# Graph layer 3: running maximum inside the gather, reciprocal in blocks beside the second pass, one message column of eight on ScalarE

## The chip, the cores and the metric

One Trainium2 chip, one of its cores. The metric is the device time of one launch in microseconds (us); lower is better. The engines are TensorE (PE in the rows; PEld is its weight load), VectorE (DVE), ScalarE (ACT), GpSimd (POOL) and SyncE (SP); SyncE and ScalarE also issue plain DMAs, GpSimd issues the indirect ones.

## The reference, cut to what matters

Four graph layers run one after the other on 3125 nodes and 100000 edges sorted by destination. The change is in the fourth, layer 3, a GATv2 attention with 4 heads of 64 numbers:

```python
def _gatv2(x, edge_index, W_l, b_l, W_r, b_r, att, bias_gat):
    xl = (x @ W_l + b_l).reshape(N, H, C)
    xr = (x @ W_r + b_r).reshape(N, H, C)
    e = jax.nn.leaky_relu(xl[src] + xr[dst], NEG_SLOPE)
    score = jnp.einsum('ehc,hc->eh', e, att)
    m = jax.ops.segment_max(score, dst, num_segments=N)
    ex = jnp.exp(score - m[dst])
    denom = jax.ops.segment_sum(ex, dst, num_segments=N)
    alpha = ex / jnp.maximum(denom[dst], 1e-16)
    out = jax.ops.segment_sum(alpha[:, :, None] * xl[src], dst, num_segments=N)
    return out.mean(axis=1) + bias_gat
```

So for each edge and head: a score, the softmax of the scores over the edges with the same destination, and the sum of the weighted source rows per destination.

## The kernel before, in words

**Layout.** Partition p holds the edges p*784 to p*784+783, one per column. Eight columns (K) are a group, 98 groups (NG) are a pass. `score` is 128 x 4 x 784: one row of 784 for each head. `f3` has the same shape.

**The gather pass** (first pass of layer 3). GpSimd fetches for each group the source rows with 8 indirect DMAs (`gather3` L814, issue at L714). SyncE loads the destination side (`load_group` L620). ScalarE writes the gathered rows out again for the second pass (`keep3a` L1087). On VectorE `edges3` (L2268) works on three groups at once: for group g it fills the destination rows column by column (`fill` L1769, instruction at L1775); for g-2 it takes the two halves that TensorE has summed (`add_up` L1338) through the leaky relu (`relu3`, L2251), adds the linear part (L2262) and reduces (L2258); for g-3 it writes the 32 finished scores (`score3`, L2266). There are 4 slots of rows: the gather of group g waits until TensorE has summed g-4 and VectorE has done both `relu3` halves of g-4, and so does SyncE's load.

**The softmax in between** is all of VectorE's steps from L2285 to L2304, one after the other (`step` waits for each): `segment_totals(6, ...)` scans the maximum forward along the columns, one scan of 784 for each head, joins the partitions and scans back; the scores less the maximum go through ScalarE's exp (L1095); `segment_totals(8, ...)` does the same with the sum. Then f3 is clamped (L2301), inverted (L2302) and multiplied into `score` (L2303), each over all 3136 columns.

**The second pass.** SyncE loads the kept rows of a group, 1 MB (`load3c` L651, four slots). The 8 columns of messages, row times weight, are made by VectorE (columns 0 to 4, KD = 5, L2322) and GpSimd (columns 5 to 7, `messages3` L822, L826) into one of two buffers `y3`. TensorE sums the four heads of the group into a PSUM bank (`head_sum` L1420, L1428, 8 recorded matmuls a group). VectorE then adds what is carried in (`sum_in`, L2033) and scans the sum of g-2 (`sum_up`, L2043) in the middle of the products of g. ScalarE copies the marks that reset the scan (L1008) and, every two groups, the finished states (`keep_states` L992, L996), and issues their DMA (L998). The products of g wait for `heads3` of g-2, which frees their `y3` buffer; `head_sum` of g waits for all products of g.

`quads` (L126) runs each pass: 6 groups written out, then a hardware loop over bodies of 4 groups. In the loop the places in `score` are computed by register instructions (DVEq, ACTq, POOLq in the rows) ahead of an instruction. `Beats` (L92) counts instructions on a semaphore; its `done` waits for the last one.

## Time and profile before

| | us |
|---|---|
| median of 3 runs | 7694.43 (7693.56 to 7702.85) |
| the profiled execution | 7678.81 |
| its span, first to last instruction | 7677.1 |
| gather pass of layer 3, 98 groups (5815 to 7078) | 1263 |
| softmax in between (7078 to 7163) | 85 |
| second pass, 98 groups (7163 to 7556) | 393 |
| rest of layer 3 (7556 to 7677) | 121 |

The profile is of one execution; stages are cut at the first and last instruction of the lines named above. "Idle before, releaser" says how long an engine had stood still before an instruction, and what ended it; "issue" is time in which nothing that the profile shows was waited for, "remote" is a semaphore event without a recorded sender.

### The profile page before, as it was taken

What the parts mean: (1) busy time and instruction counts of PE and PEld (TensorE: products, weight loads), DVE (VectorE), ACT (ScalarE), POOL (GpSimd) and SP (SyncE); (2) the same over time, 40 slices, a digit from 0 to 9 for tenths busy, and PEclk for the clock granted to TensorE, in tenths of its full rate; (3) what the DMA queues carried; (4) which work ended last, traced back from release to release, by engine and by line L of the source; (5) the groups of instructions that cost most, each with busy time, mean ns of one, the idle gap of its engine ahead of it and who ended that gap; (6) DMA issues with size and microseconds to landing.
All of it is one profiled execution on the core that took longest, in us unless ns stands there. A gap on an engine that the chain in (4) does not pass through costs nothing. (4 is left out here: it accounts for less than half of the span.)

```text
span 7677.1 us, 62689 instructions
## 1 busy us (share of the span) xinstructions
PE 2797.3 (36%) x10695; PEld 1388.6 (18%) x10695; DVE 3910.7 (51%) x10477; ACT 1035.7 (13%) x2409; POOL 3543.8 (46%) x3645
## 2 busy tenths in 40 slices
PE   2116200156600000290003333333345566555695
PEld 1114100012200000280001111111122222222232
DVE  4127200499700000299865455555545666666995
ACT  0000000012100000281352111111110000000232
POOL 5650577300177777400002655555536566654453
PEclk9999999987755555595556666666677877877897
DMA  8100000046321111100242656565637777776593
GB/s 310 44 22 13 10 1 0 0 180 231 115 85 47 47 47 47 26 0 0 101 148 71 227 198 202 196 206 193 203 110 241 243 246 244 248 245 208 208 332 117
DMA packets 458298, 1038.78 MB, mean 135 GB/s; under 512 B 129581, under 2 KB 247829, under 8 KB 428140
## 3 DMA queue, kind: packets, MB, share of 16 engines
q1 hardware_dynamic: 167594, 579.38, 21.3%
q0 software_dynamic: 131968, 217.09, 10.3%
q10 hardware_dynamic: 158658, 241.42, 8.9%
q8 instruction: 31, 0.51, 0.0%
q14 instruction: 47, 0.39, 0.0%
HBM read 559.03 MB, written 476.15 MB: 135 GB/s over the span
## 5 line engine op out<-in xcount | busy, mean ns | idle before, releaser
L714 POOL DMA_INDIRECT arena<-tab,ring x2352 | 2345.6, 997 | 1385.1 <-issue 1132.3
L1347 PE MATMUL psum<-arena,ident 128*128 128x512 f32 x1176 | 759.7, 733 | 1437.0 <-DVE arena L1775 1270.8
L1775 DVE SCALAR_TENSOR_TENSOR arena<-arena,ns 128x64 f32<-128x64 f32 (+2 forms) x2351 | 874.4, 372 | 488.2 <-issue 316.0
L756 POOL DMA_INDIRECT weights<-arena x784 | 772.6, 985 | 386.5 <-issue 332.9
L1907 DVE SCALAR_TENSOR_TENSOR arena<-iota_row,base,psum 128x200 f32<-128x200 f32 x784 | 278.3, 420 | 1083.5 <-remote 1022.5
L1348 PE MATMUL psum<-arena,ident 128*128 128x512 f32 x1176 | 696.2, 677 | 0.0
L1311 PE MATMUL psum<-agg,arena 128*128 128x200 bf16 x2352 | 262.4, 267 | 1049.5 <-issue 554.3
L1347 PEld LDWEIGHTS psum<-arena,ident 128*128 128x128 f32 x1176 | 255.5, 232 | 1832.0 <-issue 1325.6
L703 POOL DMA_INDIRECT put<-arena,zidx x75 | 73.6, 982 | 755.1 <-DVE arena L1882 646.5
L1311 PEld LDWEIGHTS psum<-agg,arena 128*128 128x128 bf16 x2352 | 210.8, 104 | 1087.3 <-issue 599.8
L2251 DVE SCALAR_TENSOR_TENSOR arena<-psum,rowb 128x1024 f32<-128x1024 f32 x196 | 239.0, 1219 | 306.7 <-remote 290.3
L1428 PE MATMUL psum<-arena,ident 128*128 128x512 f32 x784 | 361.7, 607 | 64.1 <-DVE arena L2322 63.7
L826 POOL TENSOR_TENSOR arena<-arena,score 128x256 f32<-128x256 f32 x294 | 232.5, 816 | 272.0 <-issue 121.9
L1565 DVE SCALAR_TENSOR_TENSOR arena<-psum,arena,upper 128x128 bf16<-128x128 f32 x784 | 227.3, 348 | 224.7 <-remote 171.2
L1348 PEld LDWEIGHTS psum<-arena,ident 128*128 128x128 f32 x1176 | 264.8, 225 | 365.5 <-issue 365.5
L2149 DVE SCALAR_TENSOR_TENSOR arena<-arena,ns 128x64 f32<-128x64 f32 x783 | 220.6, 282 | 193.0 <-issue 179.3
L1727 DVE TENSOR_TENSOR nodev<-psum,nodev 128x25 f32<-128x25 f32 x98 | 17.4, 178 | 549.3 <-remote 548.3
L1229 PE MATMUL psum<-arena 128*128 128x25 bf16 x784 | 38.3, 185 | 686.6 <-DVE arena L1737 565.4
L2153 DVE SCALAR_TENSOR_TENSOR arena<-arena,neg 128x64 f32<-128x64 f32 x783 | 218.3, 279 | 136.3 <-issue 126.4
L731 POOL DMA_INDIRECT arena<-betas,eidx x25 | 24.9, 995 | 569.6 <-DVE score L2025 559.2
L932 ACT ACTIVATE psum<-psum,own_row 128x512 f32<-128x512 f32 x196 | 129.8, 662 | 1119.3 <-remote 1068.3
L2258 DVE TENSOR_REDUCE arena<-arena 128x8 f32<-128x512 f32 x392 | 265.3, 678 | 0.1
(422 smaller groups left out, 4669.6 us busy)
## 6 DMA issues: line engine op xcount, KB each, us to landing
put<-zero SPq DMA_DIRECT2D x98, 1040.0 KB
arena<-put SPq DMA_DIRECT2D x98, 1040.0 KB
spill<-arena ACTq DMA_DIRECT2D x98, 1024.0 KB
arena<-spill SPq DMA_DIRECT2D x98, 1024.0 KB
state<-arena ACTq DMA_DIRECT2D x147, 512.0 KB
weights<-zero SPq DMA_DIRECT2D x32, 1600.0 KB
arena<-weights SPq DMA_DIRECT2D x32, 1600.0 KB, 7.5
put<-zero SPq DMA_DIRECT2D x14, 3584.0 KB
```

Of the source, the lines that this page charges most:

```text
L714: pool.indirect_dma_start(out=rows[:, h, k, :], out_offset=None, in_=table[:, :], in_offset=bass.IndirectOffsetOnAxis(ap=ring[:, h, word + ...
L756: pool.indirect_dma_start(out=weights0[:, :], out_offset=bass.IndirectOffsetOnAxis(ap=words0[:, g, k:k + 1], axis=0), in_=words0f[:, g, K ...
L826: message = pool.tensor_tensor(y3[:, s % 2, k, :].rearrange("p (h c) -> p h c", c=D), gc3[:, s, k, 0:HD].rearrange("p (h c) -> p h c", c=D ...
L1311: mm = pe.matmul(bank(2 + 2 * h + k // 2)[:, k % 2 * NT * R:(k % 2 + 1) * NT * R], lhsT=picks[:, h, k, :], rhs=s_parts[:, a, :], start=(a ...
L1347: pe.matmul(place, lhsT=ident[:, :], rhs=rows_of[0][:, s, columns, 0:width], start=True, stop=False)
L1348: mm = pe.matmul(place, lhsT=ident[:, :], rhs=rows_of[1][:, s, columns, 0:width], start=False, stop=True)
L1428: mm = pe.matmul(bank(h).rearrange("p (c k) -> p k c", k=K), lhsT=ident[:, :], rhs=y3[:, h, :, head * D:(head + 1) * D], start=(head == 0) ...
L1565: marked = dve.scalar_tensor_tensor(out=alike[:, h * 4 + k, :], in0=bank(h)[:, k * P:(k + 1) * P], scalar=key[:, column], in1=upper[:, :], ...
L1775: beats.add(dve.scalar_tensor_tensor(out=rows[:, s, k, :], in0=before, scalar=mark(ns, g, k), in1=rows[:, s, k, :], op0=ALU.mult, op1=ALU. ...
L1907: pick = dve.scalar_tensor_tensor(out=sifted[:, h * 4 + k, :], in0=iota_row[:, :], scalar=src_column[:, column], in1=bank(2 + 2 * h + k // ...
L2251: beats3.add(dve.scalar_tensor_tensor(out=pr3[:, columns, :], in0=bank(4 * h + 2 * part, 2).rearrange("p (k c) -> p k c", c=HD), scalar=0. ...
L2258: beats3.add(dve.tensor_reduce(rs3[:, columns, :], pr3[:, columns, :].rearrange("p k (h c) -> p k h c", c=D), AX.X, ALU.add))
```

## The change

- The forward scan of the maximum goes into the gather pass. `edges3` calls a new `maximum3(g-3)` behind column 6: it waits for `scored` and for its own four scans of the group before, then makes four scans of 8 columns into f3, each started from f3's last column. `segment_totals(6, ...)` gets `scanned=True` and makes no forward scan. The last three groups are scanned behind the pass.
- Clamp, reciprocal and product no longer run over all 3136 columns at once: the first 10 groups (6 + AHEAD3, 320 columns over the heads) are done before the second pass, the other 88 by `normalise3` in `edges3c`, in 44 blocks of two groups (64 columns), after the products of each even group, four groups ahead. `normed3` tells GpSimd and ScalarE how far it is.
- Of the 8 message columns VectorE makes 4 instead of 5 (KD = 4), GpSimd still makes 3 (now columns 4 to 6), and ScalarE makes column 7 with four activations of 64 numbers, one for each head, in its own `messages3`: that of an even group ahead of the copy of the marks, that of the odd group behind it and ahead of `keep_states`. TensorE and SyncE also wait for ScalarE's `made3c`.
- `quads(dve, edges3c, apart=AHEAD3)` writes the last four groups out on VectorE.

```diff
-KD = 5
+KD, KP = 4, 7
...
             def load3c(g, s, uses):
...
+                    sp.wait_ge(made3c, g - 3)
...
                 ready((loaded[s], uses[0] * 16 + 16 * (1 + after(3, s))), *(((heads3, g - 1),) if late(g, 2) else ()))
-                for k in range(KD, K):
+                pool.wait_ge(normed3, max(uses[1], 1) if isinstance(g, int) else uses[1])
+                for k in range(KD, KP):
...
+            def messages3(g, s, uses):
+
+                act.wait_ge(loaded[s], uses[0] * 16 + 16 * (1 + after(3, s)))
+                act.wait_ge(normed3, max(uses[1], 1) if isinstance(g, int) else uses[1])
+                if late(g, 2):
+                    act.wait_ge(heads3, g - 1)
+                for k in range(KP, K):
+                    for head in range(H):
+                        message = act.activation(y3[:, s % 2, k, head * D:(head + 1) * D], gc3[:, s, k, head * D:(head + 1) * D],
+                                                 ACT.Copy, scale=score[:, head, bass.ds(g * K, K)][:, k:k + 1])
+                message.then_inc(made3c, 1)
...
                     if s % 2:
                         return
+                    messages(g, s, uses)
                     if late(g, 4):
                         act.wait_ge(work, (g - 2) * 2)
...
+                    messages(g + 1, s + 1, uses)
                     if late(g, 2):
                         keep_states(use, work, run, table, rows, g - 2, (s - 2) % 4, before_of(g, s, uses, 2))
...
+            def maximum3(g):
+
+                dve.wait_ge(scored, g + 1)
+                maxes3.group(g)
+                maxes3.wait()
+                at = bass.ds(g * K, K)
+                for h in range(H):
+                    before = -BIG if isinstance(g, int) and g == 0 else f3[:, h, bass.ds(g * K - 1, 1)]
+                    maxes3.add(dve.tensor_tensor_scan(f3[:, h, at], neg[:, at], score[:, h, at], before, ALU.add, ALU.max))
...
+                    if late(g, 3) and k == 6:
+                        maximum3(g - 3)
...
-            step(dve.tensor_scalar(f3, f3, 1e-16, None, ALU.max))
-            step(dve.reciprocal(f3, f3))
-            step(dve.tensor_tensor(score, score, f3, ALU.mult))
+            shares3 = cin[:, 0:H * 2 * K].rearrange("p (h k) -> p h k", h=H)
...
+            def normalise3(use, first):
+
+                at = bass.ds(first * K, 2 * K)
+                eases3.group(use)
+                eases3.done(dve.tensor_scalar(shares3, f3[:, :, at], 1e-16, None, ALU.max))
+                dve.sem_inc(eased3, 1)
+                eases3.k += 1
+                eases3.add(dve.reciprocal(shares3, shares3))
+                eases3.wait()
+                eases3.done(dve.tensor_tensor(score[:, :, at], score[:, :, at], shares3, ALU.mult))
+            lead = slice(0, (6 + AHEAD3) * K)
+            step(dve.tensor_scalar(f3[:, :, lead], f3[:, :, lead], 1e-16, None, ALU.max))
+            step(dve.reciprocal(f3[:, :, lead], f3[:, :, lead]))
+            step(dve.tensor_tensor(score[:, :, lead], score[:, :, lead], f3[:, :, lead], ALU.mult))
+            dve.sem_inc(normed3, (6 + AHEAD3) // 2 - 1)
...
+                if not isinstance(g, int) and s % 2 == 0:
+                    normalise3(uses[1] - 3, g + AHEAD3)
+                    dve.sem_inc(normed3, 1)
+            quads(dve, edges3c, apart=AHEAD3)
```

## Rows read from the trace of the kernel before

**Rows 1.** Busy time by stage of layer 3: gather pass, softmax, second pass, rest.
```profile
core 0: us, PE busy (x) PEld busy (x) DVE busy (x) ACT busy (x) POOL busy (x), PEclk, DMA share, GB/s
5815.00:7078.00 1263.00, 754.98 (x1551) 316.55 (x1549) 810.50 (x1550) 0.00 (x0) 747.42 (x764) 0.80 0.73 241
7078.00:7163.00 85.00, 2.55 (x8) 1.04 (x8) 78.29 (x66) 4.38 (x5) 0.00 (x0) 0.50 0.13 49
7163.00:7556.00 393.00, 361.68 (x784) 141.74 (x784) 363.45 (x687) 145.82 (x97) 232.50 (x294) 0.99 0.89 315
```

**Rows 2.** Timeline of the softmax on VectorE: the parts that the change touches.
```profile
7078.06 7.27 DVE L1924 TENSOR_TENSOR_SCAN arena<-neg,score 128x784 f32<-128x784 f32 x4
7085.37 0.17 DVE L1972 COPY tails<-arena 128x4 f32<-128x4 f32 x1
...
7137.31 1.79 DVE L2301 TENSOR_SCALAR arena<-arena 128x3136 f32<-128x3136 f32 x1
7139.13 19.75 DVE L2302 RECIPROCAL arena<-arena 128x3136 f32<-128x3136 f32 x1
7158.92 3.43 DVE L2303 TENSOR_TENSOR score<-score,arena 128x3136 f32<-128x3136 f32 x1
7162.77 0.27 DVE L2306 MEMSET arena<- 128x256 f32 x1 [0.42 <-DVE score L2303]
```

**Rows 3.** Timeline: small VectorE instructions elsewhere in the kernel, near the new sizes.
```profile
1566.80 0.21 DVE L1744 TENSOR_TENSOR_SCAN nodev<-ones,nodev 128x25 f32<-128x25 f32 x1
...
7609.83 0.22 DVE L2354 TENSOR_SCALAR arena<-psum 128x64 f32<-128x64 f32 x1 [0.90 <-PE psum L1438]
7610.09 1.82 DVE L2355 TENSOR_TENSOR agg<-agg,arena 128x1600 f32<-128x1600 f32 x1
...
7618.07 0.55 DVE L2361 RECIPROCAL arena<-arena 128x64 f32<-128x64 f32 x1 [0.38 <-ACT arena L1099]
7618.66 0.23 DVE L2362 TENSOR_TENSOR arena<-arena,rowb 128x64 f32<-128x64 f32 x1
7618.92 1.82 DVE L2363 TENSOR_TENSOR agg<-agg,arena 128x1600 f32<-128x1600 f32 x1
```

**Rows 4.** Timeline of the second pass, one pair of groups, on VectorE.
```profile
7361.13 1.06 DVE L2322 TENSOR_TENSOR arena<-arena,score 128x256 f32<-128x256 f32 x3
7362.12 0.33 DVE L2033 SCALAR_TENSOR_TENSOR psum<-arena,ns,psum 128x64 f32<-128x64 f32 x1
7362.36 1.36 DVE L2322 TENSOR_TENSOR arena<-arena,score 128x256 f32<-128x256 f32 x2
7363.64 1.21 DVE L2043 TENSOR_TENSOR_SCAN arena<-arena,psum 128x512 f32<-128x512 f32 x1
7364.77 0.73 DVE L2322 TENSOR_TENSOR arena<-arena,score 128x256 f32<-128x256 f32 x2
7366.02 0.42 DVE L2322 TENSOR_TENSOR arena<-arena,score 128x256 f32<-128x256 f32 x1 [0.52 <-PE psum L1428]
```

**Rows 5.** The same pair on ScalarE, GpSimd and TensorE.
```profile
7361.33 2.07 ACT L996 ACTIVATE arena<-arena 128x1024 f32<-128x1024 f32 x1 [4.13 <-DVE arena L2043]
7363.56 0.34 ACTq L998 DMA_DIRECT2D state<-arena  x1
7364.36 0.95 ACT L1008 ACTIVATE arena<-ns 128x896 f32 x1 [0.96 <-ACT arena L996]
...
7361.83 2.37 POOL L826 TENSOR_TENSOR arena<-arena,score 128x256 f32<-128x256 f32 x3 [1.27 <-PE psum L1428]
7366.06 2.39 POOL L826 TENSOR_TENSOR arena<-arena,score 128x256 f32<-128x256 f32 x3 [1.86 <-issue]
...
7362.09 7.34 PE L1428 MATMUL psum<-arena,ident 128*128 128x512 f32 x16 [0.54 <-DVE arena L2322]
7369.97 1.55 PE L1428 MATMUL psum<-arena,ident 128*128 128x512 f32 x3 [0.55 <-DVE arena L2322]
```

**Rows 6.** The products' line: durations min/median/max, register instructions (DVEq).
```profile
L2322 DVE TENSOR_TENSOR arena<-arena,score x490: 391/425/847, 7163.2 to 7550.8; 128x256 f32<-128x256 f32 x164
L2322 DVEq FUSED_REGOPS  x460: 57/57/81, 7188.1 to 7548.4; - x154
```

**Rows 7.** The chain in order of time where VectorE resumes after a wait.
```profile
7365.80 0.03 issue
7365.82 0.02 DVEq L2320
...
7365.89 0.07 DVEq L2322
...
7366.02 0.07 DVE arena L2322
```

**Rows 8.** Timeline of layer 2: eight ScalarE activations of 64 numbers.
```profile
5011.81 2.02 ACT L1043 ACTIVATE arena<-arena 128x64 f32<-128x64 f32 x8
```

**Rows 9.** Timeline of the gather pass on VectorE, one burst to the next.
```profile
6552.48 1.22 DVE L2251 SCALAR_TENSOR_TENSOR arena<-psum,rowb 128x1024 f32<-128x1024 f32 x1
...
6560.82 1.23 DVE L2251 SCALAR_TENSOR_TENSOR arena<-psum,rowb 128x1024 f32<-128x1024 f32 x1
...
6568.15 0.47 DVE L1775 SCALAR_TENSOR_TENSOR arena<-arena,ns 128x260 f32<-128x260 f32 x1
6570.20 0.21 DVE L2266 TENSOR_TENSOR score<-arena 128x32 f32 x1 [1.58 <-issue]
6573.03 0.49 DVE L1775 SCALAR_TENSOR_TENSOR arena<-arena,ns 128x260 f32<-128x260 f32 x1 [2.61 <-issue]
6583.00 1.23 DVE L2251 SCALAR_TENSOR_TENSOR arena<-psum,rowb 128x1024 f32<-128x1024 f32 x1 [9.48 <-remote]
```

**Rows 10.** The same stretch on GpSimd: last gather of a burst, first of the next.
```profile
6578.02 0.95 POOL L714 DMA_INDIRECT arena<-tab,ring  x1 [0.30 <-issue]
6587.25 0.94 POOL L714 DMA_INDIRECT arena<-tab,ring  x1 [8.29 <-DVE arena L2251]
```

**Rows 11.** What ended VectorE's idle time before the relu line, whole pass.
```profile
  remote: 290.3, 32
```

**Rows 12.** Register instructions of the score line, durations in ns.
```profile
L2266 DVEq ALU_OP  x23: 17/40/1395, 5909.1 to 7056.7; - x23
```

More of the change, by code:

```diff
@@ L73 @@
 STEPS3 = 7
+AHEAD3 = 4
 READS3 = 3
-KD = 5
+KD, KP = 4, 7
 AREA = 27780
@@ L396, in gnn_program @@
         filled3, summed3, work3, scored = (sem(n) for n in ("filled3", "summed3", "work3", "scored"))
-        made3, made3b, heads3, work3c = sem("made3"), sem("made3b"), sem("heads3"), sem("work3c")
+        made3, made3b, made3c, heads3, work3c = (sem(n) for n in ("made3", "made3b", "made3c", "heads3", "work3c"))
+        maxed3, normed3, eased3 = sem("maxed3"), sem("normed3"), sem("eased3")
         resets, state_rows = sem("resets"), sem("state_rows")
@@ L998, in keep_states, with pass_sums @@
                 act.dma_start(group_rows(table, g, 2), rows[:, s:s + 2, :, :].rearrange("p a k d -> p (a k) d")).then_inc(states_out[s], 16)
-            def pass_sums(use, work, run, reset, table, rows):
+            def messages3(g, s, uses):
[8 more added lines that the diff above has]
+                message.then_inc(made3c, 1)
+            def pass_sums(use, work, run, reset, table, rows, messages):
                 def marks_and_states(g, s, uses):
@@ L1095, in _ @@
                 act.activation(score[:, r, :], score[:, r, :], ACT.Exp).then_inc(soft_exp, 1)
-            pass_sums(1, work3c, run3, reset3, state3, st3)
+            pass_sums(1, work3c, run3, reset3, state3, st3, messages3)
             act.wait_ge(root_in, 13)
@@ L1424, in head_sum @@
                 pe.wait_ge(made3b, g + 1)
+                pe.wait_ge(made3c, g + 1)
                 if not isinstance(g, int) or g >= 2:
@@ L1962, in over_partitions, with segment_totals @@
                 dve.sem_inc(c_in, 1)
-            def segment_totals(use, values, totals, n, op, marks, last_marks, spare, at_end, ends=lambda: first_last[:, :], ready=None):
+            def segment_totals(use, values, totals, n, op, marks, last_marks, spare, at_end, ends=lambda: first_last[:, :], ready=None, scanned=False):
                 neutral = -BIG if op == "max" else 0.0
                 ops = (ALU.add, ALU.max) if op == "max" else (ALU.mult, ALU.add)
-                for r in range(n):
+                for r in range(0 if scanned else n):
                     if ready:
@@ L2266, in score3 @@
                 dve.tensor_tensor(score[:, :, bass.ds(g * K, K)].rearrange("p h k -> p k h"), rs3, zl3, ALU.add).then_inc(scored, 1)
+            maxes3 = Beats(dve, maxed3, H)
+            def maximum3(g):
[6 more added lines that the diff above has]
+                    maxes3.add(dve.tensor_tensor_scan(f3[:, h, at], neg[:, at], score[:, h, at], before, ALU.add, ALU.max))
             def edges3(g, s, uses):
@@ L2290, in _ @@
                 score3(g)
-            dve.wait_ge(scored, NG)
+            for g in range(NG - 3, NG):
+                maximum3(g)
+            dve.wait_ge(maxed3, NG * H)
             for s in range(4):
                 dve.wait_ge(kept[s], 16 * (2 * groups_at(s) - 1))
-            segment_totals(6, score, f3, H, "max", neg[:, :], lambda: neg_last[:, :], spare3, lambda: penalty(late3))
+            segment_totals(6, score, f3, H, "max", neg[:, :], lambda: neg_last[:, :], spare3, lambda: penalty(late3), scanned=True)
             for r in range(H):
@@ L2300, in _ @@
             segment_totals(8, score, f3, H, "sum", ns[:, :], lambda: nl[:, :], spare3, lambda: first_last[:, :], ready=lambda r: dve.wait_ge(soft_exp, 3 + r + 1))
-            step(dve.tensor_scalar(f3, f3, 1e-16, None, ALU.max))
-            step(dve.reciprocal(f3, f3))
-            step(dve.tensor_tensor(score, score, f3, ALU.mult))
+            eases3 = Beats(dve, eased3, 4)
+            shares3 = cin[:, 0:H * 2 * K].rearrange("p (h k) -> p h k", h=H)
[13 more added lines that the diff above has]
+            dve.sem_inc(normed3, (6 + AHEAD3) // 2 - 1)
             dve.sem_inc(ended, 1)
@@ L2328, in edges3c @@
                         sum_up(1, sums3, run3, reset3, sums_of(s), g - 2, (s - 2) % 4, before_of(g, s, uses, 2))
-            quads(dve, edges3c)
+                if not isinstance(g, int) and s % 2 == 0:
+                    normalise3(uses[1] - 3, g + AHEAD3)
+                    dve.sem_inc(normed3, 1)
+            quads(dve, edges3c, apart=AHEAD3)
             for g in (NG - 2, NG - 1):
```

## The prediction

> **What bounds the kernel now.** I read the stages first [rows 1]: the change lies in the softmax (85 us), the second pass (393 us) and the gather pass (1263 us). The softmax is VectorE alone, busy 78.3 of 85 us, so each microsecond taken out of it there is gained. The three steps that go are plain to see [rows 2]: the forward scans of the maximum last from 7078.06 to 7085.37, 7.3 us; clamp, reciprocal and product from 7137.31 to the memset at 7162.77, 25.5 us, of which the reciprocal is 19.75.
>
> In the second pass VectorE is busy 363 of 393 us by the records, TensorE 362, and DMA 0.89 [rows 1]; shares don't decide here, so I read one pair of groups. TensorE's bursts start at 7362.09 and 7369.97, a pair takes 7.88 us [rows 5]. VectorE stands still for 0.52 us once in the pair, ahead of the odd group's first product, and waits there for TensorE to free the buffer; TensorE stands still 0.55 us and waits for VectorE's last product [rows 4, 5]. It is a loop of two buffers: neither has more than half a microsecond of slack in a pair, and VectorE works for 7.36 us of it.
>
> In the gather pass GpSimd issues an indirect DMA every 1.25 us (0.95 and 0.30), ten us for a group [rows 10]. VectorE takes 8.34 us for one (relu to relu, 6552.48 to 6560.82) [rows 9]. But it doesn't go on like that: GpSimd issues for three groups, waits 8.3 us for the relu, and starts again [rows 10]. Near the end of a burst VectorE goes slowly: single small instructions have 1.58 and 2.61 us in front of them, then the relu comes after 9.48 us idle, released 4.0 us after GpSimd's last issue (6578.02 + 0.95 to 6583.00) [rows 9, 10]. There are 32 such stops [rows 11], and in them a register instruction that has a median of 40 ns takes up to 1395 [rows 12]. I know the stretch from the rows, not its cause.
>
> **The change, part by part.**
>
> *Softmax, out of the path.* The forward scan loses 7.3 us. In its place stand 12 scans of 8 columns behind the pass, for the last three groups. A scan of 25 columns takes 0.21 us [rows 3] and one of 784 takes 1.82 [rows 2], 2.1 ns a column, so 0.17 for 8; 12 x 0.17 = 2.1. Gain 5.2. Clamp, reciprocal and product over 320 columns instead of 3136: the reciprocal is 0.55 at 64 columns [rows 3] and 6.25 ns for each further one, 0.55 + 256 x 0.00625 = 2.15; the product 0.23 + 256 x 0.00104 = 0.50; the clamp 0.3; with the gaps of rows 2 another 0.5. That is 3.5 for 25.5, gain 22.0. Sum: -27.2 us.
>
> *Second pass, VectorE.* The fifth product goes: three of them start within 0.99 us (7361.13 to 7362.12) [rows 4], 0.33 each, 0.66 a pair. What is left is 7.36 - 0.66 = 6.70 us. To it comes the block. Its three instructions cost, start to start at just this size, 0.26 (clamp), 0.59 (reciprocal) and 0.26 (product) [rows 3], 1.11 in all. Each waits for the one before, and register instructions and two plain increments stand in between. What that costs I take from the place where VectorE resumes after a wait: from TensorE's end at 7365.80 to the product at 7366.02, 0.22 us with two register instructions [rows 7]. Before the change these steps lie beside the running products or in the 0.52 us of idle time; behind the block's last wait nothing covers them. Bounds: all hidden, block 1.1; three such resumptions exposed, 1.1 + 3 x 0.2 = 1.7. I take 1.7, because the block is a chain of waits and resembles rows 7 more than the running products of rows 4. A pair is then 6.70 + 1.7 = 8.4 us.
>
> *Second pass, ScalarE.* Four activations cost 4 x 0.25 = 1.0 us a group [rows 8]. There is room (3.0 us busy in a pair [rows 5]), but the order counts. The even group's column stands behind the copy of the states and its DMA: from L996 at 7361.33 to the next free moment at 7364.36 are 3.03 us [rows 5], then 1.0. The column is ready at about 7365.4, where VectorE's four products would be ready at 7365.2 (the last of five ends at 7365.50 [rows 4]). So ScalarE, not VectorE, starts TensorE there. It makes a loop of its own: the odd scan's end (0.3 before the pair's end), 0.1, 3.03, 1.0, 0.25 to TensorE, 3.93 until the next product (7362.09 to 7366.02) [rows 4, 5], which is twice the pair less the pair: a pair can't be shorter than about 8.0 us. So the removed product gains nothing, and the block decides.
>
> *GpSimd and SyncE.* GpSimd's three products and SyncE's load stay; the waits on `normed3` are two to four groups early, `made3c` is ready long before the slot is. Nothing queued behind them is late.
>
> *Sum of the second pass.* 44 pairs have a block: 44 x (8.4 - 7.88) = +23; the ten groups without one may give 1 back. +22, bounds +5 (8.0) and, with the port below, +58.
>
> *Gather pass.* Four scans of 0.17 = 0.7 us at least, at most twice that, as each has three or four operands that move with the group and the products' line shows nearly one register instruction for one such operand [rows 6]. 1.0 a group, so 9.3 us beside GpSimd's 10. The scans stand behind the second relu half, on which GpSimd and SyncE wait, so after a stop they don't delay the restart. What is queued behind them is the fill of column 7, which TensorE waits for, with a group of slack. I take +3; the bounds are 0 (below nothing I see no way, as nothing is removed) and the second rival's +64.
>
> Altogether -27.2 + 22 + 3 = -2 us, on the profiled execution 7678.81 to 7677. The three runs lie 15 us above that execution; I carry the difference over to their median: 7694.43 - 2 = **7692**.
>
> **A rule of the skill.** A product that meets GpSimd's takes 847 ns, one that doesn't 391 to 425 [rows 6]: 0.43 more, once a group. The Trainium skill (SBUF — State Buffer, "SBUF: two separate sides") says that VectorE with two SBUF inputs, or in a two-port mode, and GpSimd exclude one another for a whole instruction. By that rule clamp and product of the block could each wait for a GpSimd product, 0.80 us (2.39 / 3) each.
>
> **The rivals.**
>
> *The block hides* (faster). If the register steps run beside the 0.55 us reciprocal and the 0.52 us idle time is still there to take them, a pair is 8.0, ScalarE's bound: +5. Sum -27 + 5 + 1 = -21, 7673. For it speaks that the block is put just where VectorE idles, against it that its chain is longer than that gap.
>
> *The slow stretch* (slower). Once in a burst the scans of a group fall where small instructions take 0.7 us and more. The burst's third group reaches column 6 just there [rows 9]. Some 16 instructions more are then not done when the stretch ends, and about 2 us of work, a quarter of a group's 8.34, are left ahead of the relu for which GpSimd waits. It decides as soon as that backlog outlasts the 4 us between the last issue and the release. 32 x 2 = +64 us; -27 + 22 + 64 = +59, 7753. Against it: 9.48 us idle in front of the relu are there to take it up.
>
> *The port* (slower). The block meets GpSimd's products, which start when TensorE has freed a buffer, at the block's time. 0.43 to 0.8 more in a pair: 44 x = +19 to +35; sum about +25, 7719.
>
> **How the numbers follow.** Forecast (own range 7675 to 7710) 0.36; block hidden 0.29; slow stretch 0.19; port 0.16. The range runs from the hidden block with some gain in the gather pass to just under the slow stretch in full: 7660 to 7748. 0.2% is 15 us, about what a measurement of this kernel can tell from no change. Faster: 0.29 and a tenth of the forecast's, 0.33. Within: three quarters of the forecast's and the lower ends of the two slower ones, 0.32. Slower: the rest, 0.35.
>
> **What would show it.** The softmax between the last score and the first product of the second pass at 58 us (right) or over 65 (wrong). The pair in the second pass at 8.4: 8.0 is the first rival, 8.8 the port, then with products or clamps over 0.6 us inside the block. ScalarE's column ending after VectorE's fourth product in even groups shows the ScalarE loop. The gather pass at 1263 to 1270, with 32 stops: more than 1290, or a stop that ends later than 4 us behind GpSimd's last issue, is the slow stretch. Wrong altogether it is if the block costs under 1.1 us, or if the number of groups in a burst changes.

## The result, and the profile after

| | before | after |
|---|---|---|
| median of 4 runs each, us | 7698.64 (7693.56 to 7708.93) | 7775.78 (7755.43 to 7782.42) |
| ratio | | 1.0099, interval 1.0085 to 1.0114 |
| the profiled execution's span | 7677.1 | 7772.2 |
| gather pass of layer 3 | 1263 | 1340.3 |
| softmax in between | 85 | 58.0 |
| second pass | 393 | 422.3 |
| rest of layer 3 | 121 | 121.6 |

The change makes the kernel slower by 77 us; 7692 was forecast, and the time lies above the range. The stages of the profiled execution, which answer to [rows 1] (busy time by stage, the same columns):

```profile
core 0: us, PE busy (x) PEld busy (x) DVE busy (x) ACT busy (x) POOL busy (x), PEclk, DMA share, GB/s
5830.00:7170.30 1340.30, 752.77 (x1550) 313.40 (x1548) 878.82 (x1930) 0.00 (x0) 748.54 (x765) 0.80 0.69 227
7170.30:7228.30 58.00, 2.55 (x8) 1.04 (x8) 51.08 (x74) 4.38 (x5) 0.00 (x0) 0.50 0.19 72
7228.30:7650.60 422.30, 362.86 (x784) 142.37 (x784) 382.32 (x720) 239.76 (x489) 208.27 (x294) 0.99 0.85 293
```

+77.3 in the gather pass, -27.0 in the softmax, +29.3 in the second pass: +80. The two profiled executions differ by 95 us; the other 15 lie ahead of layer 3, in code that the change doesn't touch (GpSimd's first gather of the layer is at 5789.8 before and 5805.1 after), and the medians show only 77. So the gather pass makes the loss: the softmax and the second pass together were forecast at -5 and came to +2, the gather pass was forecast at +3 and came to +77.

**Softmax.** VectorE's timeline, what answers to [rows 2]: twelve scans of 8 columns, and clamp, reciprocal and product over 320 columns.

```profile
7170.30 2.14 DVE L2297 TENSOR_TENSOR_SCAN arena<-neg,arena,score 128x8 f32<-128x8 f32 x12
...
7224.39 0.33 DVE L2350 TENSOR_SCALAR arena<-arena 128x320 f32<-128x320 f32 x1
7224.75 2.15 DVE L2351 RECIPROCAL arena<-arena 128x320 f32<-128x320 f32 x1
7226.94 0.49 DVE L2352 TENSOR_TENSOR score<-score,arena 128x320 f32<-128x320 f32 x1
```

2.14, 0.33, 2.15 and 0.49 us stand where 2.1, 0.3, 2.15 and 0.50 were worked out.

**Gather pass.** VectorE at the end of one burst, to be read beside [rows 9]:

```profile
6263.20 0.49 DVE L1794 SCALAR_TENSOR_TENSOR arena<-arena,ns 128x260 f32<-128x260 f32 x1 [1.73 <-issue]
...
6267.41 0.23 DVE L2297 TENSOR_TENSOR_SCAN arena<-neg,arena,score  x1 [3.12 <-issue]
6269.51 0.74 DVE L2297 TENSOR_TENSOR_SCAN arena<-neg,arena,score  x3 [1.87 <-issue]
...
6272.25 1.22 DVE L2270 SCALAR_TENSOR_TENSOR arena<-psum,rowb 128x1024 f32<-128x1024 f32 x1
...
6278.52 0.63 DVE L2297 TENSOR_TENSOR_SCAN arena<-neg,arena,score  x4
```

and GpSimd at the same time, beside [rows 10]:

```profile
6264.81 0.95 POOL L717 DMA_INDIRECT arena<-tab,ring  x1 [0.30 <-issue]
6276.44 0.95 POOL L717 DMA_INDIRECT arena<-tab,ring  x1 [10.68 <-DVE arena L2270]
```

A burst is a run of GpSimd's gathers without a stop; the slow stretch is the part at its end in which VectorE's small instructions are slow. Outside the slow stretch four scans take 0.63 us. In it 3.12 us of "issue" stand ahead of the first and 1.87 ahead of the second, and in 4 of 30 bursts all four start 2.1 to 2.9 us apart. The relu no longer waits: it stands straight behind VectorE's own backlog, 7.4 us after the start of GpSimd's last gather, where it was released after 5.0 before [rows 9, 10]. GpSimd stands still 10.68 us for 8.29. Over the pass there are 31 stops of over 6 us as before, with a median of 11.54 us from gather to gather for 8.93, and all stops together, each again from gather to gather (40 of over 2.5 us for 38), make 373.5 us for 298.0: +75 of the +77. The waits of VectorE in the pass, in total (us, times, longest):

```profile
DVE arena L2297 <- issue: 203.2, 92, 3.8
DVE arena L1794 <- issue: 179.4, 136, 2.3
DVE arena L2270 <- remote: 33.2, 2, 24.1
```

The relu's 290.3 us in 32 waits [rows 11] have become 33.2 in 2; 203.2 us stand ahead of the scans instead, and the fills of the destination rows (L1794) wait 179.4 us, 101.4 before.

**Second pass.** One block and the product behind it on VectorE, and ScalarE, GpSimd and TensorE in the same group:

```profile
7444.73 0.39 DVE L2372 TENSOR_TENSOR arena<-arena,score 128x256 f32<-128x256 f32 x1
7445.05 0.18 DVE L2343 TENSOR_SCALAR cin<-arena 128x64 f32 x1
7445.38 0.55 DVE L2346 RECIPROCAL cin<-cin 128x64 f32<-128x64 f32 x1 [0.15 <-DVEq L2344]
7446.07 0.41 DVE L2348 TENSOR_TENSOR score<-score,cin 128x64 f32 x1
7446.94 0.90 DVE L2372 TENSOR_TENSOR arena<-arena,score 128x256 f32<-128x256 f32 x1 [0.46 <-DVE score L2348]
...
7444.40 1.06 ACT L1012 ACTIVATE arena<-arena,score 128x64 f32<-128x64 f32 x4 [1.13 <-issue]
...
7445.78 1.78 POOL L830 TENSOR_TENSOR arena<-arena,score 128x256 f32<-128x256 f32 x3 [2.39 <-issue]
...
7445.69 3.69 PE L1447 MATMUL psum<-arena,ident 128*128 128x512 f32 x8 [0.27 <-ACT arena L1012]
```

From clamp to the next product it is 1.89 us here and 1.73 in the next block, in turns over the pass. A pair takes 8.57 us from TensorE start to TensorE start (7.89 before). ScalarE's column ends at 7445.46, VectorE's fourth product at 7445.12, and it is ScalarE that starts TensorE; so it is in every even group of the loop, by 0.34 and 0.08 us in turns. The block's product, 0.22 us when it meets nothing, takes 0.41 here, because GpSimd is in the middle of a product (7445.78 to 7446.41): VectorE's ends 0.08 us after GpSimd's.

### The profile page after: what moved, and what is told of

Read it like the earlier page. It is cut to its first block and busy times, and to the rows that moved or that the text cites. A ratio compares the mean times of both kernels' runs of the same rounds, so it can differ in the third digit from the quotient of the medians.

```text
span 7772.2 us, 65173 instructions
## 1 busy us (share of the span) xinstructions
PE 2777.7 (36%) x10695; PEld 1379.1 (18%) x10695; DVE 3970.1 (51%) x10899; ACT 1129.4 (15%) x2801; POOL 3543.8 (46%) x3645
## 5 line engine op out<-in xcount | busy, mean ns | idle before, releaser
L1365 PE MATMUL psum<-arena,ident 128*128 128x512 f32 x1176 | 745.5, 721 | 1538.6 <-DVE arena L1794 1384.8
L1794 DVE SCALAR_TENSOR_TENSOR arena<-arena,ns 128x64 f32<-128x64 f32 (+2 forms) x2351 | 872.2, 371 | 575.1 <-issue 403.9
L759 POOL DMA_INDIRECT weights<-arena x784 | 791.6, 1010 | 367.7 <-issue 314.6
L1366 PE MATMUL psum<-arena,ident 128*128 128x512 f32 x1176 | 688.6, 671 | 0.0
L1447 PE MATMUL psum<-arena,ident 128*128 128x512 f32 x784 | 362.9, 608 | 70.1 <-DVE arena L2372 63.2
L830 POOL TENSOR_TENSOR arena<-arena,score 128x256 f32<-128x256 f32 x294 | 208.3, 736 | 300.8 <-issue 167.2
L2277 DVE TENSOR_REDUCE arena<-arena 128x8 f32<-128x512 f32 x392 | 265.1, 678 | 24.5 <-issue 21.9
L2270 DVE SCALAR_TENSOR_TENSOR arena<-psum,rowb 128x1024 f32<-128x1024 f32 x196 | 238.6, 1217 | 55.6 <-remote 33.2
```

The lines of the kernel that those rows point to most:

```text
L759: pool.indirect_dma_start(out=weights0[:, :], out_offset=bass.IndirectOffsetOnAxis(ap=words0[:, g, k:k + 1], axis=0), in_=words0f[:, g, K ...
L1365: pe.matmul(place, lhsT=ident[:, :], rhs=rows_of[0][:, s, columns, 0:width], start=True, stop=False)
L1366: mm = pe.matmul(place, lhsT=ident[:, :], rhs=rows_of[1][:, s, columns, 0:width], start=False, stop=True)
L1447: mm = pe.matmul(bank(h).rearrange("p (c k) -> p k c", k=K), lhsT=ident[:, :], rhs=y3[:, h, :, head * D:(head + 1) * D], start=(head == 0) ...
L1794: beats.add(dve.scalar_tensor_tensor(out=rows[:, s, k, :], in0=before, scalar=mark(ns, g, k), in1=rows[:, s, k, :], op0=ALU.mult, op1=ALU. ...
L2270: beats3.add(dve.scalar_tensor_tensor(out=pr3[:, columns, :], in0=bank(4 * h + 2 * part, 2).rearrange("p (k c) -> p k c", c=HD), scalar=0. ...
```

## The experiments

The comparisons are always with runs of the kernel before on the same chip. That matters here: the chips are of two sorts. On the one of the result, B and C the kernel before takes 7637 to 7699 us, on the other three (D, E, F) 5021 to 5023, with the same instructions. B to F are five different chips; which one the result was measured on isn't known, and it may be C, whose time is nearest. On B and C no trace of the kernel before was taken, so stage times there are set beside those of the first chip. Gather pass times below are from the first gather to the last relu: 1284.2 us before and 1361.4 after on the first chip. The softmax is counted from the last relu to the first product (89.1 us before), and the second pass is cut 2 us shorter than in the table (391.2 before). "Stops" are from gather to gather, in the median.

### The forward maximum alone, in four forms (chip B, before 7637.08)

**max_only.** `maximum3` at column 6 as in the change, everything else as before.

```
+                    if late(g, 3) and k == 6:
+                        maximum3(g - 3)
...
-            segment_totals(6, ..., lambda: penalty(late3))
+            segment_totals(6, ..., lambda: penalty(late3), scanned=True)
```

> The kernel before, and of the whole change only the forward maximum in the gather pass: four scans of eight columns a group behind column 6, the four full scans gone from the softmax. Theory (slow stretch): the scans are the whole of the loss in the gather pass. In the changed kernel the pass from its first gather to its last relu is 1361.3 us for 1284.3, +77, and here it should be the same; the softmax gains 7.3 - 2.1 = 5.2. Sum +72, 7699 -> 7771 us, with stops of GpSimd of about 11.5 us for 9. Rival (the loss comes from the rest of the change, or upstream and by chance): within 10 us of the kernel before.

Measured: 7702.9, ratio 1.0090 (1.0072 to 1.0108), +66. Gather pass 1346.1 (1271 to 1277 in the two kernels below), stops 11.3 us, softmax 83.8 for 89.1. So the scans by themselves make the loss; the rival falls. Of the 77 us of the gather pass they account for 69 to 75, against the two kernels below.

**max_early.** The same with `k == 3`.

> The same scans, but behind column 3 (straight behind the second relu half) instead of column 6. In the trace of the changed kernel a scan outside the slow stretch starts 0.1 to 0.2 us after the one before it, inside it 2.1 to 2.8 us, and the stretch begins some 5 us behind a relu. Theory (instructions in the slow stretch): moved ahead of it they cost only what they displace; gather pass +0 to +25 for +77, total 7694 to 7719. Rival (VectorE's added time, wherever it stands, is what delays the relu): as with the scans behind column 6, 7771. Second rival (the stretch moves with the work, since something that VectorE does starts it): also near 7771, with the scans again at 2 us and more apart.

Measured: 1.0052 (1.0036 to 1.0069), +38; gather pass 1320.4. Neither size was right. VectorE behind a relu:

```profile
6209.40 1.22 DVE L2252 SCALAR_TENSOR_TENSOR arena<-psum,rowb 128x1024 f32<-128x1024 f32 x1
6211.06 0.23 DVE L2279 TENSOR_TENSOR_SCAN arena<-neg,arena,score  x1 [0.45 <-issue]
6213.19 0.23 DVE L2279 TENSOR_TENSOR_SCAN arena<-neg,arena,score  x1 [1.89 <-issue]
6214.61 0.23 DVE L2279 TENSOR_TENSOR_SCAN arena<-neg,arena,score  x1 [1.19 <-issue]
6217.41 0.23 DVE L2279 TENSOR_TENSOR_SCAN arena<-neg,arena,score  x1 [2.56 <-issue]
```

The stretch has moved with the scans: its first slow instruction comes 13.2 us after the start of the burst in the median (18.3 before, 13.6 in max_only). That is the second rival's sign, though not its size. One thing is cheaper than at column 6: after a stop the scans of the released group run while GpSimd is still waiting, so of three sets in a burst two are left to pay for, and 38 + 5 of the softmax against 66 + 5 is near two thirds. This last reading fits but wasn't tested by itself.

**wide.** One scan a group, of head s over the 32 columns of groups g-6 to g-3, once for `first` in place of four for h.

```
-                at = bass.ds(g * K, K)
-                for h in range(H):
...
+                at = bass.ds(first * K, 4 * K)
...
+                        maximum3(s, g - 6, None, g - 3)
```

> Forward maximum in the gather pass behind column 6, but one scan a group in place of four: of one head, over the 32 columns of four groups, each head in its turn. As many columns are scanned, by a quarter of the instructions. Theory (the price is by the instruction): one scan in the slow stretch is some 2.5 us, and 9.5 us of idle time stand ahead of the relu to hide it; four of them were 2.5 us too many. So the gather pass is within 5 us of the one before and the total 7694 (5 us gained in the softmax). Rival (the price is by the work, columns or busy time): four times 0.2 us against one of 0.25, a third of +77, total 7720.

Measured: 0.9995 (0.9985 to 1.0005), gather pass 1276.9, stops 8.96 us. As many columns for a quarter of the instructions add nothing to the pass. But the scan isn't free. The relu behind the burst, on VectorE:

```profile
6162.87 1.22 DVE L2252 SCALAR_TENSOR_TENSOR arena<-psum,rowb 128x1024 f32<-128x1024 f32 x1 [2.50 <-remote]
```

In the median of the 31 long stops 3.1 us of idle time are left in front of the relu, for 8.1 before: one scan, with 3.1 recorded instructions a group more, has used 5.0 us of the cover. Four scans, with 12.4 more, used all 8.1 and lengthened the stop by 2.4 to 2.6, some 10.7 in all. So the price in the stretch doesn't go by the columns, and it isn't strictly by the instruction either: a quarter of the instructions took about half the time.

**rest.** The change without its scans in the gather pass.

> The changed kernel with the forward maximum taken back into the softmax as four full scans: what is left is the reciprocals in blocks, the lead of four groups and ScalarE's column. Theory: softmax -22, second pass +29 (8.58 us a pair for 7.89), gather pass as before: +7, 7706 us. Rival (part of the gather pass's loss has to do with the rest, say with the length of the code): over 7720.

Measured: 0.9988 (0.9975 to 1.0001), 7629.62. Gather pass 1271.0, so nothing of the loss belongs to the rest. Softmax -21.9, second pass 408.0 us: +17, not +29. The pairs alternate here between 8.17 and 8.49 us; the block runs from clamp to product in 1.61 and 1.76:

```profile
7399.67 0.18 DVE L2339 TENSOR_SCALAR cin<-arena 128x64 f32 x1
7400.00 0.55 DVE L2342 RECIPROCAL cin<-cin 128x64 f32<-128x64 f32 x1 [0.15 <-DVEq L2340]
7400.70 0.23 DVE L2344 TENSOR_TENSOR score<-score,cin 128x64 f32 x1
7401.28 0.42 DVE L2368 TENSOR_TENSOR arena<-arena,score 128x256 f32<-128x256 f32 x1 [0.36 <-DVE score L2344]
```

The block's product takes 0.23 here: it starts at 7400.70, 0.06 us ahead of a GpSimd product (7400.76), where the one above starts in the middle of one. Of the 44 blocks of this kernel 20 start inside a GpSimd product, and each of these ends 0.08 us after it; two that start 0.01 us behind GpSimd's start take 0.69 us, three times their own length. Why the same instructions settle in another rhythm in this kernel stays open. The expectation was +7 in the total, -7 was measured, mostly for this reason.

### A count of instructions? (chips D, E, F, then C)

In the traces of the first chip and of B the stretch began, in the median of a kernel, when VectorE had executed 80 to 85 recorded instructions since the start of the burst (before, after, max_only, wide, rest), though the time was 18.3 us in one and 13.6 in the other. That gave the theory of these kernels. The medians hide a spread: in single bursts it was mostly 56 to 92.

**base, nops, straight, depth3** (chip D).

```
nops:      +                        for n in range(12):
           +                            dve.sem_inc(idle3 if n < 6 else idle3b, 1)
straight:  -            quads(dve, edges3)
           +            for g in range(NG):
           +                edges3(g, g % 4, (g // 4, g // 2))
depth3:    -   (work3, (g - 4) * STEPS3 + READS3)
           +   (work3, (g - 3) * STEPS3 + READS3)
```

> The kernel before, unchanged, for its trace on the same chip as the other three: gather pass of layer 3 (first gather to last relu) about 1275 us, VectorE slow from 18.3 us after the start of a burst, a stop of GpSimd of 8.9 us in three groups.

> The kernel before with twelve plain increments of semaphores that nobody waits for, on VectorE behind column 6 of each group: no work, no operand, no data, but as many instructions as the four scans with their register instructions (12.7 records a group more). Theory (a count of instructions): in the traces so far the slow stretch begins when VectorE has executed 80 to 83 recorded instructions since GpSimd began its burst, whether that is 18.3 us (before) or 13.7 us (with the scans) after it. So here it begins at 13 to 15 us, the stop grows from 8.9 to 11 us or more, gather pass +60 to +80, total +60 to +80. Rival (the scans' own work or their access to SBUF brings the stretch forward): an increment takes 0.05 us outside the stretch, 0.6 us a group, so within 15 us of the kernel before, the stretch from 18 us.

> The kernel before with VectorE's loop over the gather pass of layer 3 written out for all 98 groups: the same operations in the same order, but without the 20 register instructions a group (of 37 recorded). Theory (a count of instructions): some 17 are left a group, 51 in a burst of three, fewer than the 80 after which the stretch begins. So it doesn't begin, GpSimd's pace of 10.1 us a group sets the pass: gather pass about 1040 to 1100 us for 1275, total -180 to -240. Rival A (the stretch comes from GpSimd's issuing alone, after so many descriptors or so much time): stretch as before from 18 us, total within 20 us of the kernel before. Rival B (written-out code has to be brought in itself, and comes late): slower than before.

> The kernel before, but GpSimd gathers a group only when the relu of the group three ahead of it is done, not four: bursts of at most two groups. Theory: a burst of two groups holds 75 recorded instructions of VectorE, fewer than 80, so the stretch hardly begins; a pass of 98 groups at 20 us and a stop of 4 to 6 us for two groups is 12 to 13 us a group, 1180 to 1275 us for 1275, total -95 to 0. Rival (the stretch needs only GpSimd at work, and a shorter run-up costs): a stop of 8.9 us in two groups, 14.5 us a group, total +140 or more.

Measured: base 5023.11 (before 5021.36), nops 0.9996, straight 1.0002, depth3 1.0001, each interval with 1 in it. The expectation of base failed outright, and that is the largest finding: on this chip there is no slow stretch and no stop at all. Its gather pass (busy time by stage), and the waits of GpSimd and VectorE in it (us, times, longest):

```profile
3423.00:4417.00 994.00, 773.51 (x1552) 316.91 (x1550) 803.67 (x1543) 0.00 (x0) 749.25 (x765) 0.91 0.91 306
```

```profile
POOL arena L714 <- issue: 216.9, 712, 0.3
DVE arena L2251 <- PE psum L1348: 196.9, 64, 11.0
```

994 us for 1263, GpSimd never waits longer than its own 0.3 us between two gathers, and the relu waits for a TensorE that the records name, not for "remote". The softmax (89.1 us) and the second pass (7.89 us a pair) are the same as on the first chip to the tenth. The other three kernels say nothing about a stretch that isn't there.

**change** (chip E): the changed kernel.

> The changed kernel once more, on whatever chip comes. On a chip whose kernel before takes about 5020 us (GpSimd issues there without a stop and VectorE has no slow stretch) the theory says: gather pass as before within 3 us, since 9.3 us of VectorE lie beside 10.1 us of GpSimd a group, softmax -27, second pass +17 to +29, sum -10 to +5. Rival (the scans cost what they cost wherever they run): +60 and more. On a chip whose kernel before takes about 7640 to 7700 us: +1.0% as in the first result, gather pass +70 to +77.

Measured: 5018.74 for 5022.94, ratio 0.9992 (0.9982 to 1.0001). Gather pass 1013.3 (1018.8 in base), softmax 61.9 for 89.1, second pass 419.5 for 391.2, a pair 8.56. The scans there, and GpSimd beside them:

```profile
4002.96 0.64 DVE L2297 TENSOR_TENSOR_SCAN arena<-neg,arena,score  x4
...
4007.97 0.94 POOL L717 DMA_INDIRECT arena<-tab,ring  x1 [0.30 <-issue]
```

The softmax and the second pass are as on the first chip; the gather pass is -5 here (against base, another chip of the same sort) and +77 there. nops and straight were run again with it and with the next set, on E and F (ratios 0.9992 to 1.0003): no difference, as expected of a chip without the stretch.

**nops4, straight4** (chip C, before 7692.22): the two kernels at last on a chip that shows the stretch.

> Twelve plain increments a group on VectorE behind column 6, no work. On a chip with the slow stretch, theory (a count of instructions): the stretch begins at 13 to 15 us of the burst for 18, the stop grows from 8.9 to about 11 us, total +60 to +80. Rival (the scans' work or operands): within 15 us of the kernel before. On a chip without the stretch: no difference, as seen on three.

> VectorE's gather loop of layer 3 written out, without its register instructions. On a chip with the stretch, theory (a count of instructions): no stretch, gather pass 1040 to 1100 us for 1275, total -180 to -240. Rival (the stretch comes from GpSimd's issuing alone): within 20 us of the kernel before. On a chip without the stretch: no difference, as seen on three.

Measured: nops4 1.0000 (0.9988 to 1.0012), straight4 0.9980 (0.9969 to 0.9991), 18 us less. Both totals contradict the theory; the traces say which half of it. In straight4 VectorE has no slow instruction left in the pass. It finishes all it can do, and then stands:

```profile
6241.43 0.49 DVE L1775 SCALAR_TENSOR_TENSOR arena<-arena,ns 128x260 f32<-128x260 f32 x1
6254.81 1.23 DVE L2251 SCALAR_TENSOR_TENSOR arena<-psum,rowb 128x1024 f32<-128x1024 f32 x1 [12.88 <-remote]
...
6246.65 1.02 PE L1348 MATMUL psum<-arena,ident 128*128 128x512 f32 x2
...
6251.82 0.94 POOL L714 DMA_INDIRECT arena<-tab,ring  x1 [0.30 <-issue]
6258.96 0.94 POOL L714 DMA_INDIRECT arena<-tab,ring  x1 [6.20 <-DVE arena L2251]
```

TensorE's last recorded matmul starts before 6247.7 and by the profile's model has ended then; the relu that waits for TensorE goes on at 6254.8. Ends of matmuls are modelled, so whether the event or the end itself is late can't be told from this. Either way, in the kernel before the stop isn't VectorE's work but the lateness of that release, a median 4.7 us after the start of GpSimd's last gather and 4.5 here, with or without slow instructions; VectorE's own slowness lies hidden in front of it.

In nops4 the stretch does come early (first slow instruction at about 11 us of the burst), and where a burst still has three groups the stop grows as with the scans. VectorE and GpSimd in one such burst:

```profile
6464.80 0.68 DVE L2259 TENSOR_REDUCE arena<-arena 128x8 f32<-128x512 f32 x1
6475.40 0.49 DVE L1776 SCALAR_TENSOR_TENSOR arena<-arena,ns 128x260 f32<-128x260 f32 x1 [9.93 <-issue]
...
6477.43 1.22 DVE L2252 SCALAR_TENSOR_TENSOR arena<-psum,rowb 128x1024 f32<-128x1024 f32 x1
...
6470.44 0.94 POOL L715 DMA_INDIRECT arena<-tab,ring  x1 [0.30 <-issue]
6481.61 0.94 POOL L715 DMA_INDIRECT arena<-tab,ring  x1 [10.23 <-DVE arena L2252]
```

Twelve increments take 10 us there, and the relu comes 7.0 us after the last gather. But most bursts of this kernel have only two groups, with stops of 3 to 9 us, and 50 stops of 321.8 us in all weigh about what 38 of 298.0 weigh before (gather pass 1281.2 for 1284.2). So instructions without any work are slow in the stretch and bring it forward, as the theory says, and yet the total follows only if the rhythm of bursts stays, which the theory took for granted. This leaves a gap in the argument: by its total the rival (the scans' work or operands, within 15 us) came true. max_only records 12.4 instructions a group more and has bursts of three groups and +66 us, nops4 records 11.7 more and has mostly bursts of two and +0, on another chip. Why the rhythm differs, no run shows. depth3 wasn't run on such a chip; what shorter bursts are worth when they are forced stays open.

### The second pass, and a better version (chip F, before 5021.60; chip C, before 7692.22)

**spread.** The change with wide's scan, and the block's three instructions apart: the clamp behind the first product of the even group, the reciprocal behind its fourth, the product behind the fourth of the odd group. **spread_pool** moreover gives ScalarE's column to GpSimd (the last two lines).

```
+                    if k == 0 and not isinstance(g, int) and s % 2 == 0:
+                        normalise3(0, uses[1] - 3, g + AHEAD3)
...
-                if not isinstance(g, int) and s % 2 == 0:
-                    normalise3(uses[1] - 3, g + AHEAD3)
-                    dve.sem_inc(normed3, 1)
+                if not isinstance(g, int):
+                    if s % 2 == 0:
+                        normalise3(1, uses[1] - 3, None)
+                    else:
+                        normalise3(2, uses[1] - 3, g - 1 + AHEAD3)
...
-KD, KP = 4, 7
+KD, KP = 4, 8
```

> The changed kernel with two things placed otherwise: the forward maximum as one scan of 32 columns a group, and the block's three instructions apart (clamp behind the first product of the even group, reciprocal behind its fourth, product behind the fourth of the odd group), so that none waits for the one straight before it. Theory (the block costs 1.1 us of work and some 0.7 us of exposed waits a pair): VectorE 6.70 + 1.11 = 7.8 us a pair, ScalarE's column in the even group then sets about 8.0; second pass 391 + 5 to 8 us for 420, softmax -27, gather pass within 5 us of before: total -15 to -22 on either sort of chip. Rival (waits are hidden already, and GpSimd's products cost the difference): 8.4 and more a pair, total 0 or above.

> As the one before, but the eighth column on GpSimd instead of ScalarE (four products each for VectorE and GpSimd). Theory (ScalarE's place in the order sets 8.0): without it VectorE's 7.8 us or GpSimd's 8 products of 0.8 = 6.4 us a pair set it, 7.85 a pair, total -22 to -28. Rival (GpSimd's fourth product is what TensorE waits for, or meets VectorE's): a group 2.35 + 0.8 = 3.2 us of GpSimd behind TensorE's release, 8.2 and more a pair, total above -15.

Measured: spread 4985.5, 0.9934 (0.9918 to 0.9951); pairs of 7.76 and 8.09 us, second pass 389.0. spread_pool 4975.44, 0.9914 (0.9898 to 0.9931); pairs of 7.6, second pass 377.5. VectorE in spread_pool, over all three parts of a block (product, clamp, reciprocal, each with the product of messages behind it):

```profile
4704.43 0.21 DVE L2333 TENSOR_TENSOR score<-score,cin 128x64 f32 x1
4704.69 0.42 DVE L2359 TENSOR_TENSOR arena<-arena,score 128x256 f32<-128x256 f32 x1
...
4705.27 0.37 DVE L2327 TENSOR_SCALAR cin<-arena 128x64 f32 x1
4705.56 1.18 DVE L2359 TENSOR_TENSOR arena<-arena,score 128x256 f32<-128x256 f32 x2
...
4708.11 0.54 DVE L2330 RECIPROCAL cin<-cin 128x64 f32<-128x64 f32 x1
4708.66 0.42 DVE L2359 TENSOR_TENSOR arena<-arena,score 128x256 f32<-128x256 f32 x1
```

0.26, 0.29 and 0.55 us from start to start: 1.1 us here and 1.2 in the mean of the 44 blocks, for 1.81. In spread ScalarE's column still starts TensorE in every second even group, 0.49 us after VectorE's fourth product; in the others it ends 0.26 us before it. With GpSimd in its place VectorE's last product comes after GpSimd's in every group, and the pair is VectorE's own work. Both theories hold in their mechanism, but the gains of 36 and 46 us lie 14 and 18 us beyond their ranges: the second passes came out 7 to 10 us and some 12 us shorter than they said, and the gather passes 7 and 3 us shorter than in base. Why the gather pass shrinks is open.

**spread_pool2** (chip C):

> Block's instructions apart, forward maximum as one scan of 32 columns a group, eighth column on GpSimd. On a chip with the stretch: the one scan a group hides there as in the kernel with that part alone (+0 to +5 in the gather pass), softmax and second pass as on the other chips, total -33 to -43 of 7640 to 7700 us, 0.9945 to 0.9955. Rival (the added instructions bring a second loss there): at or above 1.0. On a chip without it: 0.991, as seen.

Measured: 7651.29, 0.9946 (0.9931 to 0.9962), gather pass 1281.7, stops 9.1 us. So this version (spread_pool) is faster than the kernel before on both sorts of chip, and by its ratio faster than the changed kernel on both. On this chip too the cover is nearly used up: 2.5 us of idle time are left ahead of the relu in the median stop, for 8.1.

## Why the prediction was wrong, point by point

**Softmax: right.** -27.2 worked out, -27.0 measured; 58 us between last score and first product were named, 58.2 are there.

**Second pass: right, a little small.** 8.4 us a pair, 8.57 measured; +22 for +29.3. Of the mis-sized 0.17 the block is 0.11: 1.81 us in the mean for 1.7, since its product starts inside a GpSimd product in 40 of 44 blocks and takes up to 0.46 us, 0.22 in the other four. The chain of waits was the right nearest row: taken apart, the same three instructions cost 1.2. The column of ScalarE ends after VectorE's fourth product, as foretold. But 8.0 isn't a floor: in spread pairs of 7.76 and 8.09 come in turns, 7.90 in the mean, and only the longer ones are started by ScalarE. The first rival, the hidden block, falls: its pair of 8.0 isn't there.

**The port, and the skill's rule: the rule holds, the meeting is rarely at its worst.** By the Trainium skill (SBUF — State Buffer, "SBUF: two separate sides") clamp and product could each wait out a GpSimd product, 0.80 us. The trace agrees with the rule: in the changed kernel all 40 block products that start inside a GpSimd product end 0.08 us after it, and in the kernel before 200 of 203 message products that do end 0.28 us after it, which is how one of 0.42 us becomes 0.85. So VectorE waits for the rest of the instruction that it meets. What the forecast's rival had too large was that rest: GpSimd's product takes 0.62 us there and was half over, which costs the block's product 0.12 to 0.24 us; the clamp meets none in the changed kernel (0.18 in all 44 blocks) and in spread costs 0.19 more (0.37). The full price shows in rest, twice, with 0.69 us for 0.22. A pair at 8.8 isn't there.

**Gather pass: this is the step that failed.** "1.0 a group, so 9.3 us beside GpSimd's 10", and +3, with the backlog of the slow stretch put away as a rival at 0.19. The rival's mechanism is what happened, with its sign as named: the stop ends later than 4 us behind GpSimd's last issue, the pass is over 1290. The forecast counted the scans at the price that they have outside the stretch, and let 9.48 us of idle time in front of the relu stand as cover for the rest. At the stretch's own price the rows nearly had the answer: the forecast's 16 instructions of 0.7 us are 11 us in a gap of 9.5. (Measured: 12.4 instructions a group, 0.91 us from one to the next in the mean, again 11 us; and the gap has a median of 8.1.) What tipped it was that I took a cover measured in idle time against a cost measured in normal time. The rival's price was low as well: 2.6 us a burst, 77 in all, for 2 and 64, because the stretch doesn't stay where it was but begins 4.5 us earlier, and more of the group's own instructions fall into it.

**What the weights missed.** The stretch isn't a property of the kernel alone. On three chips (D, E, F) it doesn't exist, and there the sum of -2 was close (-4 measured), but by luck: the second pass cost 28 for 22 and the gather pass gave back 5 where +3 was said and less than 0 was ruled out. I knew the stretch from the rows and not its cause, said so, and still gave the case in which the cause decides less than a fifth.

## What to carry to other kernels

Where an engine goes slowly in a stretch, price what you add at that stretch's rate, register instructions included, and set it against the idle time in the same stretch; a wait that hides it hides only so many instructions. Fewer and wider instructions are the cure: one scan of 32 columns stays hidden in the idle time where four of 8 cost 70 us. The rule gives the stop and not always the total: in nops4 as many instructions made the stops longer but the bursts shorter, and cost nothing. And three dependent small instructions in a row pay their waits; put between other work, they pay little more than their own time (1.2 us for 1.8).

## What was not expected of the hardware

- The same program takes 5021 to 5023 us on three chips and 7637 to 7699 on the others. The difference lies where VectorE, TensorE and ScalarE work beside GpSimd's indirect DMAs: 265 us in layer 3's gather pass (1019 for 1284), 366 to 408 in layer 2's gathers (998 for 1364 to 1406, first to last), the rest ahead of them. The second pass of layer 3, without them, takes 391 us on both.
- The largest single piece is 900 us in one stretch of the kernel before (2290 to 3266 us), where GpSimd issues 643 gathers with no pause over 0.9 us. ScalarE and VectorE wait there again and again for an event without a recorded sender; on the other sort the same stretch takes 76 us. ScalarE's row of the waits from 2290 to 3266 (us, times, longest):

```profile
ACT psum L932 <- remote: 934.2, 22, 44.0
```

- On the slow sort, from some point in a burst of GpSimd's indirect DMAs (11 to 18 us in layer 3, 6.5 in layer 2), VectorE's instructions on registers and plain increments take about 0.7 us each, and some of SyncE's (108 of 553 register instructions of the gather pass take over 0.5 us, none on the other sort); those of ScalarE, TensorE and GpSimd don't. In layer 3 it ends some 4 us behind the last gather, and a release by TensorE comes that late. Instructions without operands show it (12 increments in 10 us), so in them it isn't a matter of data or SBUF.
- The cause is open. The stretch began after 80 to 85 recorded VectorE instructions in six kernels (medians), but after 71 to 75 in max_early and nops4, and taking half of the instructions away (straight4) removes the slow instructions but not the late release. The Trainium skill (NOTIFIC — the notification-queue block, "7.1 Overflow: three behaviours, one of which stalls the engine") says that the block that writes an engine's records holds back rather than loses one inside. Whether the records themselves, which every run here was timed by, have a part in it, no run here can show.
